# A four-layer conditioned residual stack: another order of the first stage's pieces on GpSimd, VectorE, ScalarE and SyncE, and a pair of layer 0 taken ahead of T2's product

## The chip, the cores and the metric

One core of a Trainium2 chip runs the kernel. The metric is the device time of one execution in microseconds. Its matmuls run on TensorE (PE in the profile, PEld for its weight loads); VectorE is DVE, ScalarE is ACT, GpSimd is POOL, SyncE, which only issues transfers here, is SP.

## What is computed

32 samples of 64 positions and 512 features pass four layers, each with a residual. Layer 0 multiplies by a weight picked by the sample's index, layer 1 is a gated MLP (hidden width 2048) with a low-rank adapter per sample on each of its three matrices, layer 2 a linear map with an adapter, layer 3 again a weight picked per sample:

```python
x = x + einsum('bct,bcd->bdt', x, w0[idx_a]) + bias0[idx_a][:, :, None]
gate = x @ Wg + (x @ Ag[idx_a]) @ Bg[idx_a]
up = x @ Wu + (x @ Au[idx_a]) @ Bu[idx_a]
h = silu(gate) * up
x = x + h @ Wd + (h @ Ad[idx_a]) @ Bd[idx_a]
x = x + x @ W2.T + s[idx_b] * ((x @ A2[idx_b].T) @ B2[idx_b].T)
x = x + einsum('bct,bcd->bdt', x, w3[idx_c])
```

## The kernel before

Every float32 operand of layer 1 is split into a high part (a copy to the matmul's type, by ScalarE: functions ending in `_high`) and a low part (the operand less its high part, by VectorE: functions ending in `_low`). A product is then three matmuls for each 128 rows that are summed over. The gate and up products are done by a two-by-two block scheme with seven products and sums of blocks (Winograd's form of Strassen's): of the activations, blocks B11, B21, B22 and sums T1 to T4, in the slots of the tile XC; of the weights, A11, A12, A22 and S1 to S4, in WC. `XO` (L203) is the order in which XC's slots are filled, and `filled(h, slot)` the semaphore count for it. T3 and T2, T1, T4 are made by `t3_sum`, `t2_sum`, `t1_sum`, `t4_sum` on VectorE, which share two tiles.

The samples are 16 pairs (HP = 8 is half of them) in two halves; the first half's layer 1 starts while layer 0 is still computed for the second. `layer0(p)` on TensorE needs the pair's weight, which GpSimd places by two copies (`place_w0`, L539), its x, which SyncE loads (`load_xin`), and a free bank (`x1_there`: the copy of an earlier pair, `xr_copy` on ScalarE or `xr_sum` on VectorE, has run).

The adapters' input side in the first half: GpSimd selects the samples' columns (`select_a`, L587, four pieces q of four copies each, the matrices' table in RW), `a_high` and `a_low` split them, `adapters_in(0, 0)` takes q = 0 and 1, `adapters_in(0, 1)` q = 2 and 3 (after `a_sum`). `select(h, m)` on TensorE moves the result with small matrices, which GpSimd writes (`move_matrices`, one memset and four casts, semaphore `s_moves`), and `u_own` on VectorE and ScalarE masks it. The output side: the B matrices are loaded (`load_b`), split (`b_high`, `b_low`), stored in a table in DRAM (`store_b`), from which GpSimd gathers the samples' rows into the three places of BL (`gather_b`, three indirect transfers for each half). `lora` on TensorE multiplies them.

Every engine runs its instructions in the order in which its program lists them, and waits on semaphores. For the first stage these orders are written out by hand: SyncE's list of loads, GpSimd's from `pool.wait_ge(s_idx[0], 16)`, ScalarE's from `raw_high(G, 0, ...)`, VectorE's from `g_combine(0)`, TensorE's `first_gate_products` (L1829). The first products are p1 (A11 B11), p6 (S2 T2) and p5 (S1 T1) in three banks, then `c11_product`, `c21_product` and `c12_product`. In `c21_product` the lora waits for the gathered place and the product A22*T4 for `sum_u3`, which has read the same bank. After the gate's seven products come the up's seven, whose weights are combined by `p_combine(0)` on VectorE once `load_u(0)` has landed.

## Time and profile before

| | us |
|---|---|
| median of 3 runs (708.95 to 711.74) | 711.12 |
| profiled execution | 710.6 |
| its span, first to last instruction | 708.8 |
| TensorE busy | 691.5 |
| VectorE busy | 550.3 |
| GpSimd busy | 337.2 |
| ScalarE busy | 268.6 |

The span is what the profile sees; the execution's time is 1.8 us longer. TensorE is busy in 98% of the span, so that its idle pieces, 17.3 us in all, and its clock are what other engines can change. Times of single instructions are in microseconds from the span's start.

### The profile page before, as it was taken

What the parts mean: (1) busy time and instruction counts of PE and PEld (TensorE: products, weight loads), DVE (VectorE), ACT (ScalarE), POOL (GpSimd) and SP (SyncE); (2) the same over time, 40 slices, a digit from 0 to 9 for tenths busy, and PEclk for the clock granted to TensorE, in tenths of its full rate; (3) what the DMA queues carried; (4) which work ended last, traced back from release to release, by engine and by line L of the source; (5) the groups of instructions that cost most, each with busy time, mean ns of one, the idle gap of its engine ahead of it and who ended that gap; (6) DMA issues with size and microseconds to landing.
All of it is one profiled execution on the core that took longest, in us unless ns stands there. A gap on an engine that the chain in (4) does not pass through costs nothing.

```text
span 708.8 us, 10944 instructions
## 1 busy us (share of the span) xinstructions
PE 691.5 (98%) x3667; PEld 592.6 (84%) x3667; DVE 550.3 (78%) x966; ACT 268.6 (38%) x493; POOL 337.2 (48%) x614
## 2 busy tenths in 40 slices
PE   9889999999999999999999999999999999999997
PEld 7768788888888888888778888888888888799997
DVE  8777877888887878699897969696969695975553
ACT  4653513242424242334542323232323231346554
POOL 4875834444344444438356463636343433335541
PEclk9999999999999999999999999999999999999999
DMA  8779724242424232505762332322432225123332
GB/s 215 189 174 212 230 82 134 90 138 85 136 88 148 83 127 82 105 16 164 252 149 85 99 99 90 106 82 80 137 104 81 68 78 184 30 88 114 120 120 97
DMA packets 91895, 84.39 MB, mean 119 GB/s; under 512 B 44736, under 2 KB 73664, under 8 KB 91840
## 3 DMA queue, kind: packets, MB, share of 16 engines
q1 hardware_dynamic: 80128, 52.73, 25.4%
q0 software_dynamic: 11392, 30.95, 14.9%
q8 instruction: 29, 0.48, 0.3%
q14 instruction: 26, 0.21, 0.1%
q10 hardware_dynamic: 320, 0.02, 0.0%
HBM read 70.57 MB, written 13.11 MB: 118 GB/s over the span
## 4 chain that ended last, share of the span: by engine, by line
PE 82%; DVE 7%; POOL 3%; issue 3%; DMA 2%; SPq 1%; ACT 1%; POOLq 0%; DVEq 0%; ACTq 0%
PE bank L1801 40%; PE bank L1932 22%; PE bank L1809 6%; PE bank L1942 4%; PE bank L2068 3%; PE bank L2074 3%; DMA RW<-in_L_cond_Au_dram 2%; PE bank L2047 2%; PE bank L2107 2%; POOL tmp L600 1%; POOL BL L578 1%; DVE XA L1398 1%; DVE hs L1387 1%; DMA BL<-bgtab,poffs 1%; DVE hid L1381 1%
## 5 line engine op out<-in xcount | busy, mean ns | idle before, releaser
L1801 PE MATMUL bank<-XC,WC 128*128 128x512 f32 x1344 | 332.8, 394 | 4.7 <-DVE tmp L1355 2.3
L1801 PEld LDWEIGHTS bank<-XC,WC 128*128 128x128 f32 x1344 | 244.5, 189 | 51.4 <-DVE tmp L1355 3.1
L1932 PE MATMUL bank<-hs,wds 128*128 128x512 f32 x768 | 186.0, 391 | 1.0 <-DVE XA L1398 0.5
L1932 PEld LDWEIGHTS bank<-hs,wds 128*128 128x128 f32 x768 | 141.8, 188 | 29.5 <-DVE wds L1340 0.8
L578 POOL DMA_INDIRECT BL<-bgtab,poffs x96 | 99.3, 1034 | 129.5 <-PE bank L1809 91.3
L578 POOL DMA_INDIRECT BL<-butab,poffs x96 | 98.3, 1024 | 76.4 <-PE bank L1809 55.7
L877 ACT ACTIVATE hs<-hid 128x512 fp32r<-128x512 f32 x64 | 40.1, 629 | 174.7 <-DVE hid L1381 110.3
L1398 DVE TENSOR_TENSOR XA<-bank,XA 128x512 f32<-128x512 f32 x128 | 86.9, 686 | 18.5 <-PE bank L1932 16.8
L871 ACT ACTIVATE hid<-hid 128x512 f32<-128x512 f32 x48 | 30.2, 633 | 149.5 <-DVE hid L1364 79.6
L623 POOL COPY adsel<-ad_raw 128x32 f32 x256 | 46.7, 232 | 59.8 <-DVE ads L1345 59.4
L1809 PEld LDWEIGHTS bank<-UT,BL 128*128 128x128 f32 x384 | 61.5, 190 | 10.5 <-issue 2.4
L1809 PE MATMUL bank<-UT,BL 128*128 128x256 f32 x384 | 66.7, 283 | 2.2 <-DMA BL<-bgtab,poffs 2.2
L1387 DVE TENSOR_TENSOR hs<-hid,hs 128x512 fp32r<-128x512 f32 x64 | 43.8, 690 | 6.7 <-ACT hs L877 5.3
L1942 PEld LDWEIGHTS bank<-hs,ads 128*128 128x128 f32 x256 | 39.1, 189 | 5.2 <-DVE ads L1345 0.3
L1942 PE MATMUL bank<-hs,ads 128*128 128x256 f32 x256 | 40.8, 282 | 0.0
L1313 DVE TENSOR_TENSOR WC<-SC,WC 128x1024 fp32r<-128x1024 f32 x32 | 39.1, 1221 | 0.0
L1381 DVE TENSOR_TENSOR hid<-tmp,hid 128x512 f32<-128x512 f32 x48 | 33.2, 692 | 5.1 <-DVE tmp L1364 0.5
L784 ACT ACTIVATE WC<-SC 128x1024 fp32r<-128x1024 f32 x32 | 33.6, 1051 | 5.6 <-DVE SC L1300 5.6
L1351 DVE TENSOR_TENSOR tmp<-bank,tmp 128x512 f32<-128x512 f32 x32 | 22.0, 687 | 14.6 <-PE bank L1801 14.6
L861 ACT ACTIVATE tmp<-bank 128x512 f32<-128x512 f32 x32 | 19.1, 598 | 31.7 <-PE bank L1801 29.2
L1355 DVE TENSOR_TENSOR tmp<-bank,tmp 128x512 f32<-128x512 f32 x32 | 22.0, 687 | 10.3 <-PE bank L1801 10.3
L1372 DVE TENSOR_TENSOR hid<-bank,tmp 128x512 f32<-128x512 f32 x16 | 11.1, 691 | 22.2 <-PE bank L1809 22.2
(217 smaller groups left out, 867.1 us busy)
## 6 DMA issues: line engine op xcount, KB each, us to landing
RW<-in_L_cond_Wg_dram SPq DMA_DIRECT2D x16, 512.0 KB, 3.5
RW<-in_L_cond_Wu_dram SPq DMA_DIRECT2D x16, 512.0 KB, 3.4
RD<-in_L_cond_Wd_dram SPq DMA_DIRECT2D x16, 512.0 KB, 3.5
out_dram<-XB SPq DMA_DIRECT2D x15, 256.0 KB, 2.1
XB<-in_x_dram SPq DMA_DIRECT2D x8, 256.0 KB, 5.9
x1park<-XB SPq DMA_DIRECT2D x8, 256.0 KB, 6.1
x2park<-XA SPq DMA_DIRECT2D x8, 256.0 KB, 3.1
XA<-x1park SPq DMA_DIRECT2D x4, 512.0 KB, 6.4
```

The source lines that it names most:

```text
L578: nc.gpsimd.indirect_dma_start(BL[:, place, x, :].bitcast(f32), None, btab[b % 2][i], bass.IndirectOffsetOnAxis(poffs[:, at:at + 1].bitcas ...
L623: last = nc.gpsimd.tensor_copy(adsel[:, :, n // DS, n % DS * RANK:(n % DS + 1) * RANK], ad_raw[:, 2 * i:2 * i + 2, bass.ds(col, RANK)])
L784: nc.scalar.activation(WC[:, t, S1:S4 + 1, 0, :, :], SC[:, :, :].rearrange("p s (k f) -> p s k f", k=2), ACT.Copy).then_inc(s_wh[t], 1)
L877: nc.scalar.activation(hs[:, f, 0, t * 512:(t + 1) * 512], hid[:, 2 * f + t, :], ACT.Copy).then_inc(s_hh, 1)
L1313: nc.vector.tensor_tensor(WC[:, t, S1:S4 + 1, 1, :, :], SC[:, :, :].rearrange("p s (k f) -> p s k f", k=2), WC[:, t, S1:S4 + 1, 0, :, :].b ...
L1381: nc.vector.tensor_tensor(hid[:, block_, :], tmp[:, {3: 3, 2: 2, 1: 1}[block_], :], hid[:, block_, :], ALU.mult).then_inc(s_hid, 1)
L1387: nc.vector.tensor_tensor(hs[:, f, 1, at], hid[:, 2 * f + t, :], hs[:, f, 0, at].bitcast(f32), ALU.subtract).then_inc(s_hl, 1)
L1398: nc.vector.tensor_tensor(sums, psD[j % 2][:, :], sums, ALU.add).then_inc(s_evict, 1)
L1801: last = nc.tensor.matmul(psum[:, :], WC[:, t, left, a, k, :], XC[:, right, b, k, :], start=(first and k == 0 and n == 0), stop=(k == 1 an ...
L1809: last = nc.tensor.matmul(psum[:, x * P:x * P + QT], BL[:, b_place(b, tok), x, f * P:(f + 1) * P], UT[:, j, tok, x, :], start=(first and n ...
L1932: last = nc.tensor.matmul(psD[j % 2][:, :], by_feature(wds[:, f, a, :])[:, j % KT, :], hs[:, f, b, j // KT * 512:(j // KT + 1) * 512], sta ...
L1942: last = nc.tensor.matmul(psR[q // 2][:, q % 2 * QT:(q % 2 + 1) * QT], ads[:, f, q, :, :].rearrange("p a m -> p (a m)"), hs[:, f, b, q * Q ...
```

## The change

Five orders are changed. GpSimd writes the moving matrices before anything that needs the indices, places pairs 12 and 13 ahead of the adapters' selection, and selects all four pieces together, ahead of pairs 14 and 15. SyncE stores the first B table ahead of the loads of pairs 14 and 15 and of what follows them. ScalarE takes the sums of the gate's weights earlier and B21 ahead of T2, T3 right behind it. VectorE does the same with the low parts. TensorE takes `layer0(HP + 2)` ahead of p6 instead of behind it.

```diff
-        XO = [[B11, T2, B21, T3, T1, B22, T4], [B11, B21, T3, T2, B22, T1, T4]]
+        XO = [[B11, B21, T2, T3, T1, B22, T4], [B11, B21, T3, T2, B22, T1, T4]]
...
                 load_b(0)
                 for p in range(HP + 2, PAIRS - 2):
                     load_xin(p)
+                store_b(0)
                 for p in range(PAIRS - 2, PAIRS):
                     load_xin(p)
                 load_b(1)
                 load_g(1)
-                store_b(0)
                 load_idx(2, idx_c)
                 load_u(0)
...
                     if p == 0:
+                        pool.wait_ge(s_moves, 1)
                         pool.wait_ge(s_w0i, 1)
                         pool.wait_ge(s_zero, 2)
                     if p == HP:
                         pool.wait_ge(s_zero, 4)
-                    if p == HP + 4:
-                        pool.wait_ge(s_araw, 2)
...
                     if q == 0:
                         pool.wait_ge(s_al, 32 * (h + 1))
-                        pool.wait_ge(s_w0c, PAIRS if h else HP + 4)
-                    if q == 2 and h == 0:
-                        pool.wait_ge(s_w0c, PAIRS - 2)
+                        pool.wait_ge(s_w0c, PAIRS if h else PAIRS - 2)
...
+                pool.wait_ge(s_ident, 1)
+                move_matrices(0)
                 pool.wait_ge(s_idx[0], 16)
...
-                select_a(0, 0, cols)
-                select_a(0, 1, cols)
                 late += adapters(24, 8)
                 for p in range(HP + 4, PAIRS):
                     if p == PAIRS - 2:
-                        select_a(0, 2, cols)
-                        select_a(0, 3, cols)
+                        for q in range(HQ):
+                            select_a(0, q, cols)
                     place_w0(p, late[2 * (p - HP):2 * (p - HP) + 2])
                 pool.wait_ge(s_w0c, PAIRS)
-                move_matrices(0)
                 gather_b(0, 0)
...
                 xc_high(0, B11)
-                for p in range(SUMMED + 1, HP):
+                xr_copy(SUMMED + 1)
+                sums_high(G, 0)
+                for p in range(SUMMED + 2, HP):
                     xr_copy(p)
-                sums_high(G, 0)
+                xc_high(0, B21)
+                xr_copy(HP)
                 xc_high(0, T2)
-                xr_copy(HP)
+                xc_high(0, T3)
                 xr_copy(HP + 1)
-                xc_high(0, B21)
                 a_high(0, 0)
                 a_high(0, 1)
-                xc_high(0, T3)
                 xr_copy(HP + 2)
+                b_high(0)
                 xr_copy(HP + 3)
-                b_high(0)
                 xc_high(0, T1)
...
                 xc_low(0, B11)
+                sums_low(G, 0)
                 t3_sum(0)
                 t2_sum(0)
-                sums_low(G, 0)
+                xc_low(0, B21)
                 xc_low(0, T2)
-                xc_low(0, B21)
+                xc_low(0, T3)
                 a_low(0, 0)
                 a_low(0, 1)
-                xc_low(0, T3)
                 t1_sum(0)
...
                     layer0(HP)
                     layer0(HP + 1)
+                    layer0(HP + 2)
                     pe.wait_ge(s_wl[G], 1)
                     pe.wait_ge(s_xcl, filled(0, T2))
                     p6_product(0, G)
-                    layer0(HP + 2)
                     layer0(HP + 3)
```

## Rows read from the trace of the kernel before

**Rows 1.** The page's part 4: the chain that ended last, by engine.

```profile
PE 82%; DVE 7%; POOL 3%; issue 3%; DMA 2%; SPq 1%; ACT 1%; POOLq 0%; DVEq 0%; ACTq 0%
```

**Rows 2.** TensorE's longest wait from 0 to 90 us: total, times, longest.

```profile
PE bank L1809 <- DMA BL<-bgtab,poffs: 2.2, 1, 2.2
```

**Rows 3.** Timeline of TensorE: start, duration, instructions, idle before and what ended it.

```profile
23.84 1.62 PE L1801 MATMUL bank<-XC,WC 128*128 128x512 f32 x6 [1.42 <-DVE XC L1252]
...
28.23 1.69 PE L1769 MATMUL bank<-XC,UT 128*128 128x256 f32 x12
...
34.56 1.64 PE L1801 MATMUL bank<-XC,WC 128*128 128x512 f32 x6 [0.37 <-DVE XC L1252]
37.02 3.13 PE L1769 MATMUL bank<-XC,UT 128*128 128x256 f32 x24 [0.83 <-DVE UT L1329]
...
51.57 0.66 PE L1809 MATMUL bank<-UT,BL 128*128 128x256 f32 x3 [2.17 <-DMA BL<-bgtab,poffs]
52.03 2.76 PE L1801 MATMUL bank<-XC,WC 128*128 128x512 f32 x6
...
57.02 5.63 PE L1801 MATMUL bank<-XC,WC 128*128 128x512 f32 x24
```

**Rows 4.** Two stretches: length, busy us of the engines, granted clock, DMA share, GB/s.

```profile
18.00:23.80 5.80, 4.42 (x27) 3.59 (x26) 4.91 (x4) 4.07 (x6) 3.47 (x7) 1.00 0.88 215
51.60:56.00 4.40, 4.40 (x16) 3.69 (x17) 3.04 (x5) 0.63 (x1) 0.30 (x1) 0.61 1.02 125
```

**Rows 5.** Timeline of VectorE and ScalarE: t3_sum, T2's low part, a_high, a_low.

```profile
18.75 1.23 DVE L1261 TENSOR_TENSOR hid<-XA 128x1024 f32<-128x1024 f32 x1 [2.20 <-ACT XA L756]
...
22.39 1.30 DVE L1252 TENSOR_TENSOR XC<-hid,XC 128x1024 fp32r<-128x1024 f32 x1
...
26.51 0.63 ACT L809 ACTIVATE BL<-tmp 128x512 fp32r<-128x512 f32 x1 [1.75 <-POOL tmp L600]
...
27.18 0.69 DVE L1329 TENSOR_TENSOR WC<-tmp,BL 128x512 fp32r<-128x512 f32 x1 [0.85 <-ACT BL L809]
```

**Rows 6.** GpSimd's timeline, then its selection copies (ns, min/median/max), one copy alone.

```profile
5.76 1.10 POOL L551 COPY hid<-adsel 64x64 f32 x4 [3.15 <-ACT w3bd L939]
...
15.86 2.75 POOL L551 COPY w0second<-adsel 64x64 f32 x8 [0.72 <-issue]
20.84 5.64 POOL L600 COPY tmp<-RW 128x128 f32 x8 [2.23 <-DMA RW<-in_L_cond_Au_dram]
...
36.84 2.05 POOL L611 CAST WC<-ident 128x128 fp32r<-128x128 f32 x4
39.06 1.15 POOL L578 DMA_INDIRECT BL<-bgtab,poffs  x1 [0.18 <-issue]
...
L600 POOL COPY tmp<-RW x16: 287/418/1283, 20.8 to 32.3; 128x128 f32 x16
...
22.57 1.28 POOL L600 COPY tmp<-RW 128x128 f32 x1
```

**Rows 7.** Timeline of VectorE: sum_u3 of the gate.

```profile
50.04 0.68 DVE L1355 TENSOR_TENSOR tmp<-bank,tmp 128x512 f32<-128x512 f32 x1
```

**Rows 8.** p_combine's start; the store's issue; issues with us to landing; DMA rates, 0:90.

```profile
43.16 0.42 DVE L1295 TENSOR_TENSOR SC<-RW 128x256 f32<-128x256 f32 x1
...
31.54 0.38 SPq L427 DMA_DIRECT2D bgtab<-hs  x1
...
RW<-in_L_cond_Wu_dram SPq DMA_DIRECT2D x1, 512.0 KB, 6.6
...
butab<-hs SPq DMA_DIRECT2D x1, 256.0 KB, 4.9
...
BL<-bgtab,poffs POOLq DMA_INDIRECT x1, 5.2
...
GB/s 3 136 303 350 393 347 120 57 128 273 246 7 117 220 311 182 181 56 115 84 300 266 252 150 93 137 147 200 246 275 358 356 317 309 136 113 295 221 214 97
DMA packets 40584, 18.25 MB, mean 203 GB/s; under 512 B 27520, under 2 KB 37248, under 8 KB 40576
```

## The prediction

> **What bounds the kernel now.** I read four things in this order. The shares of the chain that ended last say which engine sets the time: TensorE has 82% of it [rows 1]. So only two things can move the time here, TensorE's idle time and its clock, and the diff touches only the first 50 us. The list of TensorE's waits there, and its instructions in order of time, give the idle pieces with what ended them [rows 2, 3]: 1.42 us until the low part of T2 (product p6 at 23.84), 0.37 until T1's (p5 at 34.56), 0.83 until the last adapter piece (adapters_in(0,1) at 37.02), 2.17 until the gathered BL rows (51.57). Then the table by stretches, for the granted clock: 1.00 around the 1.42 us wait, 0.61 in the stretch behind the 2.17 us wait, that is part of it at 1.2 instead of 2.4 GHz [rows 4]. The six matmuls of the A22*T4 product took 2.76 us there; its neighbours' 24 took 5.63 [rows 3]. Last, the instructions of VectorE, ScalarE and GpSimd one by one, for what feeds these four waits [rows 5 to 7], and the transfers [rows 8]. Later waits of the kernel follow from TensorE's own progress; I let them move along unchanged.
>
> **T2 and p6.** Before, p6 waited for t3_sum, t2_sum, xc_high(T2), xc_low(T2), ending 23.69 [rows 5]. The first sum waits for the copy of layer 0's eighth pair and starts at 18.75 before and after: nothing moves that. sums_low(G) moves into VectorE's 2.20 us gap ahead of it, since its ScalarE half now runs after xr_copy(5), done near 16.6. xc_low(B21) takes its place ahead of T2's, and xr_copy(HP) stands ahead of xc_high(T2), but TensorE has finished its pair before t2_sum ends. So T2's low part still ends near 23.8. What fills the wait is layer0(HP + 2), about 1.5 us of matmuls; p6 starts near 24.1, followed by layer0(HP + 3) alone, and TensorE is at adapters_in(0,0) at 27.0 instead of 28.23. That would be worth 1.2 us if the adapters' pieces were there.
>
> **GpSimd, where that gain goes.** move_matrices(0) (one memset 0.31 and four casts, 2.05 for these [rows 6]) goes into the 3.15 us in which GpSimd waited ahead of its first placement at 5.76 [rows 6]; it has the matrices done by about 5, with the index load beside it, so the placements of pairs 0 to 7 stay. I cost this at nothing; without that cover it is up to 2.4 us on layer 0's first pairs.
> The placements of pairs 12 and 13 now stand ahead of the adapters' selection. A GpSimd copy takes 0.29 us at the least, but 1.28 when VectorE is in a subtraction of 1024 columns: the copies ran one for each such instruction, each ending just behind it (the one at 22.57 under VectorE's at 22.39) [rows 5, 6]. Twelve copies now stand from 15.86. The first is held as before (16.65), the second by sums_low to 17.9, three run free to 18.8, the next five are held by t3_sum, t2_sum, xc_low of B21, T2 and T3 (20.1, 21.4, 22.5, 23.9, 25.1), two run free to 25.7. The selection begins at 25.85; before it began at 20.84, when its data landed [rows 6]. Each piece is four copies, about 1.0 us, now with VectorE idle: 26.85 and 27.8. Then a_high 0.63 and a_low 0.69 [rows 5] in turn: 27.5, 28.2, 28.5, 29.2. adapters_in(0,0) starts at 29.25, TensorE having idled 2.2 us; before it started at 28.23.
> From there TensorE has 5.9 us (adapters_in and two pairs) to p5, 35.15 against 34.56. T1's low part is ready: the selections of q = 2, 3 end near 31.95 (the copies again one for each of a_low, t1_sum, b_low), then a_sum 0.7 and xc_low(T1) 1.2 give 33.8. xc_low(B22) and two a_low end 36.2, p5 ends 36.6. So adapters_in(0,1) starts at 36.6 instead of 37.02: **0.4 us gained**, the idle 1.42 + 0.37 + 0.83 exchanged for one of 2.2. Bounds: 1.0 us worse, if also the free copies are held; if no placement is held, adapters_in(0,0) starts at 27.0 and VectorE's chain of low parts allows 2.5 us in all.
>
> **BL, the larger part.** Without move_matrices and with the selection in one piece, GpSimd ends placing at about 35.7. The rows of the table need store_b(0): it is issued when b_low(0) ends, 31.05, and its second half took 4.9 us with a 512 KB load ahead of it [rows 8], which is now behind: 36.0. The gathers start there instead of at 39.06 [rows 6]. The one that TensorE waited for was issued 7.2 us after the first one and took 5.2 us [rows 8]: 48.4. TensorE asks at 49.4 - 0.4 = 49.0. So this wait goes. Next late is VectorE's sum_u3, which starts at 50.04 behind u_own(0,5) and takes 0.68 [rows 7]; it starts from TensorE's own last selection and releases the A22*T4 product at 50.78 - 0.4. From there at full clock product, rows, product, rows are 3.5 us: the up products start at 54.3 - 0.4 against 57.02 [rows 3]. sum_c22, which frees the bank for them, moves along and is just in time. **2.7 us gained**, of it 1.2 the wait and 1.5 the clock, since one idle microsecond is left.
>
> **The store ahead of the loads.** In SP's queue store_b(0) is moved past two loads of x (512 KB), and with them load_b(1) (256 KB), load_g(1) (512 KB), the indices and load_u(0) wait for b_low(0). The x of pair 14 lands near 36, needed at 39.5. load_u(0) is needed at 42.7 (p_combine(0), before at 43.16 [rows 8]); behind it on VectorE is u_own(0,0), for which select(0,2) waits. Before, the store was issued at 31.54, the load at about 33, and it landed 6.6 later, 8.1 after the store's issue. With 1.3 MB more in between: 31.05 + 8.1 + 3.5 = 42.7 at the 350 to 390 GB/s of the best slices, 45.5 at the mean 203 [rows 8]. The backlog is dense, so I take the first, and 0.3 us of cost; range 0 to 2.8.
> The Trainium skill (DMA: Bandwidth & Descriptors, Queues, rings and completion order) says that each DMA engine consumes the descriptors of one queue in ring order, which speaks against this edit: every load issued behind the store lands behind it. If order didn't matter, load_u(0) would be in time at any rate. The landings of the trace, in order of issue, agree.
>
> **Sum.** 0.4 + 2.7 - 0.3 = 2.8. The profiled execution took 710.6 (span 708.8), which gives 707.8; the median 711.12 lies 0.5 above it: 708.3. I use the median.
>
> **Rivals.** (1) The new 2.2 us idle at 27 to 29 halves TensorE's clock. For: the 2.17 us one did, and cost about 1.6 us (from 51.57 to 57.02 it is 5.45 us for work of 3.9 at full clock); against: 1.42 us did not, and mine may be shorter. It would take back 1.6: 709.9. Chance 0.3, forecast 0.46. (2) GpSimd is held less than I say, the selection ends early, and TensorE never waits at 27. For: several copies took only 0.3 beside VectorE work; against: the copies at 1.28 [rows 6], one for each of VectorE's long instructions. Up to 2.1 more: 706.2. Chance 0.12. (3) **Slower**: load_u(0) late holds p_combine(0), u_own(0,0) and select(0,2). For: the first gathers now move beside it, and the mean rate gives 45.5. Each microsecond past 42.7 costs one; a stop as long as before's 2.17 us costs the clock's 1.6 too. It decides from a landing at about 44.9 (2.2 + 1.6 against 3.1): then 0.7 slower than before; at 46, 1.8 slower, 712.9. Against: the dense backlog. Chance 0.07 for this, 0.05 for a milder delay (709.5). (4) That the order changes nothing at all (the gathers still late, 711) is in the tails.
>
> **Chances.** 0.5% is 3.6 us, about what a measurement can tell from no change. The forecast lies 0.8 us inside; a third of its chance and most of (2) give faster 0.28; slower by that much needs (3) at its worst: 0.06; within: 0.66. The range runs from (2) to the clock case with a microsecond of delay: 706.2 to 711.2.
>
> **What would show it.** The wait of p6 gone, a wait of 2.2 us at adapters_in(0,0) at 29.2, ended by a_low; the selection starting near 25.8; adapters_in(0,1) near 36.6; the first gather near 36; no wait for BL, one of about 1 us for sum_u3, no stretch at 1.2 GHz there; up products near 54.2. Wrong would be: a DMA wait at p_combine(0), a stretch at half clock after 29, or adapters_in(0,0) ahead of 28.2.

## The result, and the profile after

The changed kernel took 713.42 us (median of 20 runs, 711.6 to 715.75); the kernel before took 710.8 beside it (20 runs, 708.95 to 712.58). The ratio is 1.0034, 95% interval 1.0025 to 1.0044: 2.4 us slower (2.6 by the two medians). The forecast was 708.3 with a range up to 711.2, so the time lies outside it, on the other side of the kernel before. The profiled execution took 714.06 us, its span 712.2, granted clock 0.992. In what follows a ratio leaves out runs that were disturbed as a whole, but a median holds them (two of a_moves_back's 12 took 3894 us, the other ten have a median of 711.26; one of the kernel before's 1381 us in batch 3 and one 1140 us in batch 5).

TensorE's timeline after (start, duration, operation, count, idle before it and what ended it; lines of the file moved up by two or three):

```profile
25.19 1.61 PE L1799 MATMUL bank<-XC,WC 128*128 128x512 f32 x6
...
30.01 1.70 PE L1767 MATMUL bank<-XC,UT 128*128 128x256 f32 x12 [1.89 <-DVE WC L1327]
...
35.92 1.64 PE L1799 MATMUL bank<-XC,WC 128*128 128x512 f32 x6
37.39 3.04 PE L1767 MATMUL bank<-XC,UT 128*128 128x256 f32 x24
...
43.19 1.11 PE L1775 MATMUL bank<-WC 128*128 128x256 f32 x7
44.14 1.55 PE L1799 MATMUL bank<-XC,WC 128*128 128x512 f32 x6
45.81 0.59 PE L1775 MATMUL bank<-WC 128*128 128x256 f32 x3
47.01 0.59 PE L1775 MATMUL bank<-WC 128*128 128x256 f32 x3 [0.61 <-issue]
47.43 0.52 PE L1807 MATMUL bank<-UT,BL 128*128 128x256 f32 x3
50.87 1.19 PE L1775 MATMUL bank<-WC 128*128 128x256 f32 x4 [2.92 <-DVE UT L1408]
51.86 2.76 PE L1799 MATMUL bank<-XC,WC 128*128 128x512 f32 x6
...
56.64 1.66 PE L1799 MATMUL bank<-XC,WC 128*128 128x512 f32 x6 [0.74 <-DVE tmp L1353]
...
60.24 2.00 PE L1799 MATMUL bank<-XC,WC 128*128 128x512 f32 x8
```

Against the kernel before [rows 3], the waits of the first part went as forecast: p6 at 25.19 and p5 at 35.92 have no wait, one wait of 1.89 us stands ahead of adapters_in(0,0), the 0.83 us at adapters_in(0,1) is gone, and so is the wait of 2.17 us for the BL rows at the LoRA products (L1807). What was not forecast stands between: from 45.81 on the matrix selections (L1775) stutter and then stop for 2.92 us, released by VectorE's u_own (L1408). The up products start at 60.24 instead of 57.02, 3.2 us late, and the rest of the kernel keeps that lag: from the start of the up products to the end of the span it is 652.0 us here and 651.8 before.

Why was u_own late? VectorE's timeline of the same execution:

```profile
43.44 0.42 DVE L1293 TENSOR_TENSOR SC<-RW 128x256 f32<-128x256 f32 x1
...
44.97 0.69 DVE L1408 TENSOR_TENSOR UT<-bank,own 128x512 fp32r<-128x512 f32 x1
50.03 1.29 DVE L1408 TENSOR_TENSOR UT<-bank,own 128x512 fp32r<-128x512 f32 x2 [4.37 <-remote]
```

The third selection's matmuls stand at 45.81 for 0.59 us, so they end at 46.40; the u_own that needs only them starts at 50.03, after VectorE had idled 4.37 us. What lies between is the signal from TensorE: its record stands at 50.01, 3.6 us after the matmuls' end. The next selection (end 47.59) and the first rows' product (47.95) are recorded at 50.06 and 50.11, almost together with it. p_combine, at 43.44, is not late (43.16 before [rows 8]), so load_u(0) is not the cause.

The stretches of the clock (length, then busy us and instructions of TensorE, its weight loads, VectorE, ScalarE, GpSimd; then granted clock, DMA share, GB/s):

```profile
7.98:11.39 3.41, 3.41 (x17) 3.41 (x17) 2.91 (x15) 1.53 (x3) 1.42 (x6) 0.50 1.02 352
...
48.94:55.76 6.82, 4.89 (x16) 4.19 (x16) 1.75 (x3) 2.09 (x6) 0.00 (x0) 0.50 1.01 147
```

Two stretches ran at 1.2 GHz (granted clock 0.50): one over layer 0's first pairs, behind a wait of 0.97 us for bias_r at 6.96, and one over the stall and what follows it; before, only the one behind the BL wait did [rows 4]. GpSimd's timeline after, the placements' copies (L550), the selection's (L597), the gathers (L577):

```profile
2.80 1.05 POOL L608 CAST WC<-ident 128x128 fp32r<-128x128 f32 x4
6.07 1.07 POOL L550 COPY hid<-adsel 64x64 f32 x4 [2.21 <-ACT w3bd L936]
...
16.15 10.17 POOL L550 COPY w0second<-adsel 64x64 f32 x12 [1.54 <-issue]
26.55 6.20 POOL L597 COPY tmp<-RW 128x128 f32 x16 [0.23 <-POOL w0second L550]
32.93 3.63 POOL L550 COPY w0second<-adsel 64x64 f32 x4 [0.18 <-POOL tmp L597]
36.86 1.28 POOL L577 DMA_INDIRECT BL<-bgtab,poffs  x1 [0.29 <-POOL w0second L550]
```

### The profile page after: what moved, and what is told of

The parts are those of the page before. It is cut to its first block, busy times and chain, and to the rows that moved or that the text cites. A ratio compares the mean times of both kernels' runs of the same rounds, so it can differ in the third digit from the quotient of the medians.

```text
span 712.2 us, 10944 instructions
## 1 busy us (share of the span) xinstructions
PE 692.7 (97%) x3667; PEld 593.9 (83%) x3667; DVE 549.6 (77%) x966; ACT 268.6 (38%) x493; POOL 337.5 (47%) x614
## 3 DMA queue, kind: packets, MB, share of 16 engines
q0 software_dynamic: 11392, 30.95, 14.8%
## 4 chain that ended last, share of the span: by engine, by line
PE 84%; DVE 8%; issue 3%; POOL 1%; POOLq 1%; ACT 1%; another core or an unknown queue 1%; DMA 0%; SPq 0%; DVEq 0%; ACTq 0%
PE bank L1799 41%; PE bank L1930 22%; PE bank L1807 6%; PE bank L1940 4%; PE bank L2066 3%; PE bank L2072 3%; PE bank L2045 2%; PE bank L2105 1%; PE bank L1767 1%; POOLq L582 1%; DVE XA L1396 1%; POOL w0second L550 1%; DVE hid L1379 1%; DVE XC L1250 1%; DVE hs L1385 1%
## 5 line engine op out<-in xcount | busy, mean ns | idle before, releaser
L577 POOL DMA_INDIRECT BL<-bgtab,poffs x96 | 98.9, 1030 | 130.0 <-PE bank L1807 91.3
L577 POOL DMA_INDIRECT BL<-butab,poffs x96 | 98.8, 1030 | 81.4 <-PE bank L1807 61.0
L1807 PEld LDWEIGHTS bank<-UT,BL 128*128 128x128 f32 x384 | 61.4, 190 | 8.0
L1807 PE MATMUL bank<-UT,BL 128*128 128x256 f32 x384 | 66.5, 282 | 0.0
L1311 DVE TENSOR_TENSOR WC<-SC,WC 128x1024 fp32r<-128x1024 f32 x32 | 38.9, 1217 | 0.0
L2066 PE MATMUL bank<-XC 128*128 128x288 f32 x192 | 28.1, 295 | 0.0
```

The lines of the kernel that those rows point to most:

```text
L577: nc.gpsimd.indirect_dma_start(BL[:, place, x, :].bitcast(f32), None, btab[b % 2][i], bass.IndirectOffsetOnAxis(poffs[:, at:at + 1].bitcas ...
L1311: nc.vector.tensor_tensor(WC[:, t, S1:S4 + 1, 1, :, :], SC[:, :, :].rearrange("p s (k f) -> p s k f", k=2), WC[:, t, S1:S4 + 1, 0, :, :].b ...
L1807: last = nc.tensor.matmul(psum[:, x * P:x * P + QT], BL[:, b_place(b, tok), x, f * P:(f + 1) * P], UT[:, j, tok, x, :], start=(first and n ...
L2066: last = nc.tensor.matmul(banks[:, first, to:to + QT + 2 * RANK], x2t[d % 2][:, a, k, at], W2A[:, b, k, 2 * RANK - w:4 * RANK - w + QT], s ...
```

## The experiments

Five batches of two to four kernels each; the kernels of one batch (the expectations say "call") ran on one chip, beside the kernel before. "Up products" is their start in the profiled execution (57.02 before). "Signals" says whether the records of TensorE's signals stand late in that execution, and whether TensorE's selections stalled with them.

A ratio is not the quotient of the medians beside it: a_again_2 has 0.9977, while its medians give 0.9988. Microseconds worked out from a ratio are good to about 1 us.

| batch | kernel | median us | ratio to before (95%) | up products | signals |
|---|---|---|---|---|---|
| 1 (before 710.91) | a_again | 712.95 | 1.0034 (1.0018 to 1.0051) | 59.00 | late |
| 1 | a_store_back | 712.5 | 1.0026 (1.0012 to 1.0040) | 57.09 | late, one wait of 1.22 |
| 1 | a_moves_back | 711.92 | 1.0014 (0.9987 to 1.0042) | 56.75 | late, no stall |
| 1 | a_ads_late | 712.94 | 1.0023 (1.0004 to 1.0042) | 59.27 | late |
| 2 (before 709.54) | a_gather_held | 710.1 | 1.0009 (0.9997 to 1.0022) | 55.75 | in time |
| 2 | a_pool_sp_back | 709.35 | 0.9997 (0.9984 to 1.0010) | 55.99 | in time |
| 2 | a_sel_moves_back | 709.88 | 1.0005 (0.9995 to 1.0015) | 54.58 | in time |
| 2 | b_moves_early | 709.37 | 0.9998 (0.9988 to 1.0007) | 56.94 | in time |
| 3 (before 710.04) | a_again_2 | 709.16 | 0.9977 (0.9966 to 0.9988) | 55.23 | in time |
| 3 | b_gathers_early | 708.31 | 0.9976 (0.9963 to 0.9989) | 54.02 | in time |
| 3 | a_third_held | 709.24 | 0.9987 (0.9975 to 0.9998) | 54.67 | in time |
| 3 | a_sel_back | 707.42 | 0.9955 (0.9942 to 0.9969) | 53.50 | in time |
| 4 (before 710.02) | a_again_3 | 708.04 | 0.9977 (0.9966 to 0.9989) | 56.80 | in time |
| 4 | b_gathers_early_2 | 708.24 | 0.9974 (0.9963 to 0.9985) | 54.90 | in time |
| 4 | a_third_held_2 | 708.33 | 0.9979 (0.9969 to 0.9990) | 54.95 | in time |
| 4 | a_sel_back_2 | 707.21 | 0.9972 (0.9960 to 0.9984) | 53.68 | in time |
| 5 (before 710.81) | a_again_4 | 712.86 | 1.0027 (1.0013 to 1.0042) | 54.64 | late, no stall |
| 5 | a_sel_back_3 | 712.9 | 1.0026 (1.0013 to 1.0040) | 59.67 | late |

The last column is worked out from the trace: for each of the 585 TensorE instructions of an execution that signal another engine, the time from the matmul's end to the recorded signal. In thirteen profiles (the twelve marked "in time" and the one of the kernel before) none comes over 0.5 us and under 4 us late between 10 and 700 us; in seven (those marked "late" and the first profile of the changed kernel) 33 to 42 do. The one profile of the kernel before is of an execution of 710.6 us that is not among the 20 of the first comparison, and the later batches have none of it; whether its signals come late beside a changed kernel whose signals do isn't known.

Where a signal's own record is missing, the count takes the next one, so 33 to 42 is an upper count. What is real is told by the engine that waits. In after, a_again, a_ads_late and a_sel_back_3 VectorE starts the third selection's u_own 3.6, 1.5, 2.9 and 2.4 us after that selection's end, each time within 0.03 us of a recorded signal. In a_store_back, a_moves_back and a_again_4 it starts 0.04 us after that end, though no record stands there: the signal came and only its record is missing.

One more reading of all twenty profiles: from the start of the up products to the end of the span it is 651.65 to 651.80 us where signals are in time and 651.77 to 652.09 where they are late. So the spans, which go from 705.3 to 712.2 us, differ by what happens ahead of the up products, and late signals behind them cost under 0.5 us.

### Batch 1: which part of the change makes the stall

a_again is the changed kernel once more.

> The changed kernel once more, nothing edited. In its first trace TensorE ends select(0,2), select(0,3) and the first rows' product by 48.0 us, but their signals reach VectorE and the others together at 50.0, and 3.5 us are lost at 47 to 51. If this belongs to the change (theory 1), this trace shows signals of TensorE that come over 1 us late between 43 and 51 again, and the ratio to the kernel before is 1.003 to 1.004. If it was an accident of that one execution (theory 2), the first up product starts near 56 instead of 60.2, though the ratio may still be 1.003 from the clock: two or more stretches at 1.2 GHz.

Both halves came: 1.0034, and the signals late (pair 15's matmuls end at 44.07, its signal is at 45.81), with a stall in two pieces, 0.90 and 1.33 us. Here the wait ahead of adapters_in(0,0) was 2.45 us and the clock did fall behind it, as rival 1 says; in the first profile, behind 1.89 us, it didn't.

a_store_back puts the store of the gate table back behind the loads:

```diff
-                store_b(0)
                 for p in range(PAIRS - 2, PAIRS):
                     load_xin(p)
                 load_b(1)
                 load_g(1)
+                store_b(0)
```

> The changed kernel with the store of the first B table back behind load_g(1), everything else as changed. If the early store, with the loads and gathers pushed into each other behind it, is what costs (theory S), the time falls by 2 us or more below the changed kernel's, to 711 or less, ratio 1.000 or below. If not, the first gathers start later by up to 1 us, still ahead of need, and the time stays within 0.7 us of the changed kernel's.

No stall at its first four selections, up products at 57.09, but 1.0026 in its timed runs: one profile doesn't speak for the runs here. The first gather was issued at 36.69 and took 2.07 us, the second stood at 39.06; then TensorE waited 1.22 us for BL. One signal did come late: the sixth selection ends at 49.13, its signal is at 50.79, and VectorE had idled for it:

```profile
50.82 0.69 DVE L1408 TENSOR_TENSOR UT<-bank,own 128x512 fp32r<-128x512 f32 x1 [3.67 <-remote]
...
52.16 2.93 PE L1799 MATMUL bank<-XC,WC 128*128 128x512 f32 x6 [1.22 <-DVE tmp L1353]
```

sum_u3 stands behind that u_own, and the A22*T4 product waits 1.22 us for it.

a_moves_back puts the zero matrices back ahead of the first gather:

```diff
                     if p == 0:
-                        pool.wait_ge(s_moves, 1)
...
-                pool.wait_ge(s_ident, 1)
-                move_matrices(0)
                 pool.wait_ge(s_idx[0], 16)
...
                 pool.wait_ge(s_w0c, PAIRS)
+                move_matrices(0)
                 gather_b(0, 0)
```

> The changed kernel with move_matrices(0) back behind the last placement. If the matrices in GpSimd's first gap cost something at the start (they held VectorE's small instructions by 0.3 us and with them the bias, theory M), the first product p1 starts 0.3 us earlier and the time falls by 0.3 us or more; otherwise the first gather starts 2.4 us later, near 39.2, and BL's wait of up to 2 us returns: 1 to 2 us slower than the changed kernel.

First gather at 38.87, BL wait 1.95, no stall. Its interval, 0.9987 to 1.0042, holds both the kernel before and a_again: it decides nothing.

a_ads_late tests whether SyncE's issue of the second Ad transfer, which took 4.3 us just where the signals are late (45.68 to 49.98), is what delays them:

```diff
                 for n in range(ADAPTERS):
+                    if n == 1:
+                        sp.wait_ge(s_prod, 6)
                     sp.dma_start(ad_raw[:, :, n * RANK:(n + 1) * RANK],
```

> The changed kernel; SyncE waits for the sixth product signal (near 50 us) before the second of the eight transfers of Ad, whose issue took 4.3 us from 45.7 to 50.0 in the changed trace, exactly until TensorE's late signals arrived. If this issue delays them (theory L), the signals come within 0.1 us of the matmuls' ends, select(0,4) follows by 47.5 instead of 50.9, and the time falls by 2.5 us or more, ratio 1.000 or below. If the cause is elsewhere, the time stays within 0.7 us, or rises when the later Ad transfers come late.

The stall stayed (0.62 and 2.18 us, up products at 59.27), with no such issue beside it. That theory falls; the same issue takes 4.0 us in the kernel before (from 45.42) and 4.9 us in a_again_2, where signals are in time.

### Batch 2: hold the gathers, and single parts

```diff
                 pool.wait_ge(s_w0c, PAIRS)
+                pool.wait_ge(s_prod, 3)
                 gather_b(0, 0)
```

> The changed kernel with one wait more: GpSimd holds its first gather until TensorE's third product of gate 0 (T1's) is through, so about 38.4 us where it was 36.3 to 36.9; the zero matrices stay first and SyncE's store stays early. Theory G (the gathers' transfers, started before 37 us beside the loads that the early store pushed back, make TensorE's signals between 43 and 50 us come late): the late signals go, the matrix selections run as one block without a stall near 46 to 50, up products start near 57.0 instead of 59 to 60.2, and the median falls by 1.5 to 2.5 us to 710.5 to 711.5. Theory P (the late signals come from what the early matrices do at the start, a TensorE that runs about half a microsecond behind the other engines throughout): the signals are late all the same, up products near 59 or later, median near 713. Either way the clock stretch behind the idle at 29 us remains.

The signals were in time and the ratio 1.0009. At the time I read this as theory G confirmed. It isn't: in the other three kernels of this batch no signal was late either, so this batch can't tell what the held gathers did to them. What it does show is the price of late gathers (the first at 39.29) where no signal is late, a BL wait of 1.34 us:

```profile
51.84 0.59 PE L1808 MATMUL bank<-UT,BL 128*128 128x256 f32 x3 [1.34 <-DMA BL<-bgtab,poffs]
```

a_pool_sp_back keeps only the orders of ScalarE, VectorE and TensorE (it undoes the hunks of GpSimd and SyncE).

> Of the change only the orders of ScalarE, VectorE and TensorE: T2 behind B21, the T2 product behind a third pair of layer 0; GpSimd's and SyncE's orders are those of before. My forecast's first term alone: T2's wait of 1.42 us goes, adapters_in(0,0) at 27.0 to 28.5, no idle over 1.5 us before it and so no half-rate stretch there; the wait for BL (2.2 us) and the half-rate stretch behind it near 52 stay as before. Theory O (the order costs nothing by itself): 710.4 to 711.2, ratio 0.999 to 1.001 to before. Rival: the order by itself is the loss, since sums_low and T3's halves ahead of a_low put back what VectorE gives a_low: adapters_in(0,0) at 29 or later, 712 to 713.

Two rows of TensorE's timeline:

```profile
28.05 1.70 PE L1771 MATMUL bank<-XC,UT 128*128 128x256 f32 x12 [1.23 <-DVE WC L1331]
...
36.04 3.14 PE L1771 MATMUL bank<-XC,UT 128*128 128x256 f32 x24 [0.44 <-DVE UT L1331]
```

adapters_in(0,1) starts 0.98 us earlier than before (37.02 [rows 3]), but the ratio is 0.9997: in the timed runs the order alone can't be told from nothing.

a_sel_moves_back undoes all of GpSimd's hunks and keeps the early store.

> The changed kernel with GpSimd's order of before in full (adapter selection behind the twelfth pair's placement, zero matrices at the end), the early store and the orders of ScalarE, VectorE and TensorE kept. The run that had only the matrices back kept a wait of 2.45 us before adapters_in(0,0) and one of 1.95 for BL. If the late selection is what makes that first wait (its copies hold VectorE while it has a_low to write), it is under 1 us here and adapters_in(0,0) starts by 28.5; first gather about 38.9, BL wait 1.5 to 2.2, up products near 56.5, median 710 to 711: the same as before or up to 0.8 us below. If the wait comes from VectorE's own order, it stays near 2 us and the median is 711.5 to 712.

adapters_in(0,0) starts at 28.40 behind 1.23 us, the BL wait is 1.92, the ratio 1.0005. Against a_moves_back's 2.45 us, with the late selection, the wait is half as long: the late selection is its source, as forecast. Behind the 1.92 us its profile has no stretch at half clock.

b_moves_early is the kernel before with the zero matrices first.

> The kernel before with one thing changed: the zero matrices and their copies ahead of the first placement. Forecast's second term alone: first gather near 37, 2 us earlier, the BL wait of 2.17 us under 0.8, up products near 56. Theory G, in the form that needs the early store as well, expects no late signals here and a gain of 1 to 2 us: 709 to 710. If early gathers alone delay TensorE's signals, a stall of 1 to 3 us stands in the selections near 46 to 50 and the median is 711 to 713. If the early copies cost VectorE its small operations (bias_r late at 7 us, half-rate stretch in layer 0's first pairs, as the changed kernel's trace had), that costs up to 1.3 us at 7 to 12 us.

```profile
39.12 1.15 POOL L579 DMA_INDIRECT BL<-bgtab,poffs  x1 [2.64 <-issue]
```

GpSimd was ready 2.64 us early and waited for the stored table: the gathers did not move (39.06 before [rows 6]). The matrices are worth nothing without the store, and with a_store_back the converse holds. Only together do they bring the gathers forward to 36.4 (b_gathers_early below).

### Batch 3: the same kernel, now faster

b_gathers_early is the kernel before with the zero matrices first and the early store, and nothing else of the change. a_third_held holds the third block of gathers, up's:

```diff
+                    if unit == 0:
+                        pool.wait_ge(s_sel, 3)
                     gather_b(b + 1, 0)
```

a_sel_back is the changed kernel with the adapters' selection where it was (the waits that go with its place are left out here):

```diff
...
+                select_a(0, 0, cols)
+                select_a(0, 1, cols)
                 late += adapters(24, 8)
                 for p in range(HP + 4, PAIRS):
                     if p == PAIRS - 2:
-                        for q in range(HQ):
-                            select_a(0, q, cols)
+                        select_a(0, 2, cols)
+                        select_a(0, 3, cols)
```

> The changed kernel, nothing altered, timed beside the three kernels of this call, because the kernel before read 1.2 us lower beside the last four than beside the first four. If the kernels of the last call were near 1.000 for what they had put back, this one stays at 1.003 (1.002 to 1.0045) and its trace shows the late signals again, with gathers from 36.3 to 36.9 on; if it reads 1.001 or less, the ratios of different calls can't be set beside one another.

> The kernel before with the zero matrices first and SyncE's store of the gate table ahead of the last inputs: with the matrices alone the first gather stayed at 39.12 after 2.64 us of idle (the table was not stored), so the two edits together are what brings the gathers to 36 to 37. ScalarE's, VectorE's and TensorE's orders and the selection's place are those of before. Theory G (the time of the gathers alone makes TensorE's signals late): a stall of 1 to 3.5 us in the matrix selections between 45 and 51, up products at 58 or later, ratio 1.002 to 1.004. Rival, that it needs the changed kernel's selection or orders too: no stall, the BL wait under 1 us, up products near 55.5, ratio 0.997 to 0.999.

> The changed kernel with the third block of gathers (up's table, the seventh to ninth, which the changed kernel issues from 45.0 to 47.5) held until TensorE has signalled its third matrix selection; the first six stay at 36.3 to 43. If it is the up table's gathers, at 45 to 48, beside the selections that make the signals late, they are in time here: no stall, no BL wait, up products near 55.5, ratio 0.998 to 1.000, and this is the version that keeps what the change was to bring. If it is the first six, the stall of 2 to 3.5 us stays and the ratio is 1.003.

> The changed kernel with the adapter selection where it was, half behind the twelfth pair's placement; zero matrices and store stay early. adapters_in(0,0) at 28.0 to 28.6 behind a wait of 1.2 to 1.4 us, as in the two runs that had this order, instead of 29.4 to 30.0 behind 1.9 to 2.45. Gathers from about 36.0 on. Theory G: the late signals and a stall of 1 to 3.5 us in the selections stay, ratio 1.001 to 1.003, a little under the changed kernel's because the path is 0.8 to 1.2 us earlier up to the stall. Rival, that the stall comes from the late start of adapters_in: none here, ratio 0.997 to 0.999.

The changed kernel, nothing altered, was faster than the kernel before: 0.9977, which is 1.6 us (0.9 by the medians). Its third selection and u_own, VectorE's row:

```profile
46.99 1.29 DVE L1408 TENSOR_TENSOR UT<-bank,own 128x512 fp32r<-128x512 f32 x2 [0.78 <-PE bank L1775]
```

and TensorE's:

```profile
7.59 1.08 PE L2002 MATMUL bank<-bias_r,bias_of 40*128 40x64 f32 x8 [1.03 <-DVE bias_r L1201]
...
30.64 1.70 PE L1767 MATMUL bank<-XC,UT 128*128 128x256 f32 x12 [1.88 <-DVE WC L1327]
...
43.81 1.11 PE L1775 MATMUL bank<-WC 128*128 128x256 f32 x7
...
46.35 0.94 PE L1775 MATMUL bank<-WC 128*128 128x256 f32 x6
47.82 0.71 PE L1775 MATMUL bank<-WC 128*128 128x256 f32 x4 [0.17 <-DVE UT L1408]
...
51.64 1.66 PE L1799 MATMUL bank<-XC,WC 128*128 128x512 f32 x6 [0.71 <-DVE tmp L1353]
...
55.23 5.63 PE L1799 MATMUL bank<-XC,WC 128*128 128x512 f32 x24
```

From the first selection to the block of four it takes 4.0 us here (43.81 to 47.82) and 7.7 in the first profile (43.19 to 50.87): the late signals cost 3.7 us. To the up products it is 11.4 against 17.1 us, so another 2.0 us go with the clock and the waits behind. The two spans differ by 5.2 us (707.0 and 712.2), and 5.0 of these stand at the start of the up products (55.23 and 60.24), though the first profile was 0.6 us ahead at the first selection. This is the path that the forecast describes: no BL wait, 0.71 us for sum_u3, full clock behind it.

b_gathers_early has up products at 54.02, 3.0 us before those of the kernel before, and 0.9976: the part that brings the gathers forward is the whole gain of the changed kernel. a_third_held (0.9987) neither helps nor hurts by an amount that its interval shows. a_sel_back, with six runs, has the lowest ratio of the study:

```profile
28.18 1.69 PE L1773 MATMUL bank<-XC,UT 128*128 128x256 f32 x12 [1.09 <-DVE WC L1333]
...
36.16 3.14 PE L1773 MATMUL bank<-XC,UT 128*128 128x256 f32 x24 [0.45 <-DVE UT L1333]
...
49.92 1.66 PE L1805 MATMUL bank<-XC,WC 128*128 128x512 f32 x6 [0.72 <-DVE tmp L1359]
...
53.50 5.63 PE L1805 MATMUL bank<-XC,WC 128*128 128x512 f32 x24
```

### Batches 4 and 5: chip or moment

> The changed kernel a third time. One of two: trace with late signals (pair 15's signal after 43.5 with its products' end over 1 us before it, up products at 59 or later) and ratio 1.002 to 1.0045; or trace without (up products near 55 to 56) and ratio 0.997 to 0.9985. Nothing in between if the stall is the whole difference.

> The kernel before with matrices first and the store early, again. Theory G (early gathers make the signals late, where the chip or the moment is such that it happens at all): it shows the stall whenever the changed kernel of this call shows it, ratio then 1.001 to 1.003, and 0.997 to 0.998 otherwise. If it goes without the stall while the changed kernel has it, the gathers' time is not enough and the orders matter.

> The third block of gathers held, again. Where the changed kernel of this call stalls: no stall here if up's gathers are the cause (ratio 0.999), the same stall if the first six are (ratio 1.003). Where it doesn't stall: 0.998 to 0.999.

> The changed kernel with the selection back where it was, again: fastest so far, 0.9955. If the stall comes: selections up to 1.2 us earlier than the changed kernel's, ratio 1.000 to 1.002. If it doesn't: 0.995 to 0.997.

Batch 4 repeats batch 3 on another chip, with overlapping intervals: 0.9977, 0.9974, 0.9979, 0.9972. No signal is late. In a_again_3's profile the wait at adapters_in(0,0) was 2.45 us and the clock stayed at half from 28.7 to 35.6. That is rival 1, and it had its price: from adapters_in(0,0) to p5 it took 8.6 us (29.44 to 38.05) against 5.9 in a_again_2 at full clock, 2.7 us more, and this execution, 710.31 us, was the slowest of the kernel's nine, whose median is 708.04.

> The changed kernel a fourth time. If the late signals go with the chip: on the chip of the first two calls ratio 1.002 to 1.0045 and a stall of 2 us or more in the selections between 45 and 51; on another chip either that, or 0.997 to 0.999 with up products at 55 to 57 and no stall. A ratio near 1.003 with no late signals in the trace, or one near 0.998 with them, would say that the stall is not what separates the calls.

> The selection back where it was, a third time: 0.9955 to 0.9972 so far. Where the changed kernel stalls in this call, this one stalls too if early gathers are enough (its first gather is at 35.9 to 36.0, as early as the changed kernel's), ratio 1.000 to 1.002; where it doesn't, 0.995 to 0.998.

Batch 5 ran on the same chip as batch 4, some minutes later, with late signals and 1.0027 and 1.0026. And batches 1 and 2, on one other chip, differ in the same way. So the chip is not what decides. Within batch 5 two of the changed kernel's 12 runs took 708.49 and 709.1 us and ten 711.4 to 714.8; the profiled one is the 708.49, which lacks records like the others, but where VectorE starts in time (up products 54.64). So none of the ten longer executions has a profile. a_sel_back_3's profile, of 713.53 us, has the stall:

```profile
44.78 0.59 PE L1781 MATMUL bank<-WC 128*128 128x256 f32 x3
46.15 0.59 PE L1781 MATMUL bank<-WC 128*128 128x256 f32 x3 [0.78 <-issue]
...
48.65 1.19 PE L1781 MATMUL bank<-WC 128*128 128x256 f32 x4 [1.54 <-issue]
49.64 2.76 PE L1805 MATMUL bank<-XC,WC 128*128 128x512 f32 x6
...
54.42 2.93 PE L1805 MATMUL bank<-XC,WC 128*128 128x512 f32 x6 [0.74 <-DVE tmp L1359]
```

It shows too that the late selection isn't needed for the stall.

Another thing goes with the late signals, in all seven profiles and in none of the thirteen: records of semaphore updates are missing. 6228 to 6316 are recorded over an execution there, against 8564 to 8571 in the others, and of the 2,299 that a_again_4 lacks against a_again_3, 1,471 (525, 519 and 427) belong to the three semaphores of the BL gathers. It can be seen without counting, in the list of DMA issues from 30 to 44 us, whose last column is the median time from issue to landing. a_again, then a_again_3:

```profile
BL<-bgtab,poffs POOLq DMA_INDIRECT x6
```

```profile
BL<-bgtab,poffs POOLq DMA_INDIRECT x6, 3.8
```

In a_again no landing could be told. The packets themselves are the same in number and median duration (11,392 of the gathers' queue in either), so the packets are not slower; what is late or lost are the messages about them, and the engines' signals beside them. TensorE's are not the only ones: in the first profile 78 of VectorE's 855 and 50 of ScalarE's 431 signals have no record within 0.3 us, in a_again_2 none. A missing record need not mean a late signal: ScalarE's masking ends at 46.86 in the first profile and the next record of its semaphore stands 6.39 us later, but TensorE, which waits for it, went on at 47.01.

## Why the prediction was wrong

**T2 and p6.** The exchange of waits was right, its balance not. p6 has no wait, and adapters_in(0,0) was expected at 29.25 behind 2.2 us; the changed kernel's five profiles give 29.44 (twice), 29.84, 30.01 and 30.64, four of them behind 1.88 to 2.45 us (a_again_4 has 1.36 us ahead of a pair at 23.92 in its place). p6 was forecast at 24.1 and stands at 24.05 in the two profiles whose clock was full up to there and that had no wait ahead of it (a_again, a_again_3). adapters_in(0,1) was to start at 36.6, 0.4 earlier than before; it started at 37.2 to 38.2, and at 39.5 in a_again_3 behind the half clock, later than the 37.02 of before. With the selection back (a_sel_back) it started at 36.16. So the T2 order is worth up to 0.9 us by the trace, and the late selection takes that and more.

**GpSimd.** The selection was forecast at 25.85, it started at 26.55, and at 25.97 in a_again_3, where the first pairs were at full clock. Twelve copies took 10.17 us, 0.85 us each against 0.29 us at the least, which agrees with VectorE's long instructions holding them. The cover of the zero matrices held: the first placement stands at 5.83 to 6.69 in the kernels that have them first, and at 5.76 to 6.21 in the four that don't. What I had not reckoned with is a clock stretch at the very start: four profiles, all of kernels with matrices, store and selection as changed, have a wait of 0.86 to 1.14 us for bias_r at 7 us and half clock from 8 or 9 us on; a_moves_back has the wait (1.19) and not the stretch, so its cause isn't settled. In the first profile p1 starts at 19.23 instead of the 18.09 of a_again, 1.1 us later; the selection's 0.7 us and adapters_in's 0.8 us against the forecast go with this stretch.

**BL and the clock.** The mechanism was right: the first gather at 36.3 to 37.5 (forecast 36), no BL wait, 0.51 to 1.02 us for sum_u3 (forecast 1), no half clock there where no signal was late. It was the last placement that released the first gather (0.29 us ahead of it), not the store, for which I had 36.0: in a_again_3 the two tables landed at 33.5 and 34.5. By the profiles the part is worth its 2.7 us: b_gathers_early's up products start 3.0 and 2.1 us ahead of 57.02. By the runs it is less: b_gathers_early measures 0.9976 and 0.9974, which is 1.7 and 1.8 us, with intervals of about 0.9 us to either side. I had put the clock's 1.5 us in full. But the kernel before hasn't its half-rate stretch in every run: three of its runs in batch 3 (709.01, 709.11 and 710.01 us) show a granted clock of 1.000 over the whole execution. The one profile that I had showed the stretch.

**The store.** The 0.3 us is in the noise. p_combine at 43.44 shows that load_u(0) was in time; in a_again_3, whose records are complete, it landed at 41.5 (forecast 42.7). The nine transfers from the store on landed there in the order of their issue, 33.5 to 41.5, as the prediction had it, without consequence. The Trainium skill (DMA: Bandwidth & Descriptors, Queues, rings and completion order) says only that descriptors are consumed in ring order, and that a later one may finish its write first; that what is issued later also lands later is what the traces show here.

**The sum.** 2.8 us were forecast; batches 3 and 4 gave 0.9977 twice, 1.6 us (0.9 and 2.0 by the medians). The BL term with the store (2.7 - 0.3 = 2.4) measured 1.75 as b_gathers_early, 0.65 less; what is left for T2 and the selection is 1.6 - 1.75 = -0.15 where the sum had 0.4, 0.55 less. These two make the missing 1.2, but each is within the intervals; the second holds the clock stretches at 8 us and behind the wait at 29, of which the latter is rival 1. In those two batches the prediction's 708.3 stands beside 709.16 and 708.04. That it is near is in part luck: the kernel before took 710.04 and 710.02 there and not the 711.12 that the forecast starts from.

**What failed outright.** The step "So this wait goes. Next late is VectorE's sum_u3", which "starts from TensorE's own last selection". It takes TensorE's signals for immediate. They were, in the only profile that I had, that of the kernel before (0 of 585 late). In four profiles of the first comparison and of batches 1 and 5 VectorE got them 1.5 to 3.6 us late in the selections, a stretch where TensorE waits for VectorE and VectorE for TensorE piece by piece, so that each late signal is on the path; TensorE stood 2.92 us and the up products started at 60.24, where my sum has 54.2. In those comparisons the changed kernel takes 712.86 to 713.42 us against 709.16 and 708.04 elsewhere, 3.7 to 5.4 us more. The kernel before takes 710.80 to 710.91 against 709.54 to 710.04, 0.8 to 1.4 us more; why is not shown, as there is no profile of those executions. None of my rivals had this, and rival 3, the only one on the slower side, had another mechanism, which no trace shows.

**What stays open.** Four things. (1) What sets one batch apart from another: not the chip, as batches 4 and 5 show. (2) Whether the changed kernel is hit harder because its gathers run from 36.3 instead of 39.06 us, and so complete among the selections' signals: for it speak that most of the missing records are the gathers', that the two kernels with one of the two edits back (gathers from 38.9, or from the second on at 39.06) had no stall at their first four selections, and their ratios of 1.0014 and 1.0026 against 1.0034; but these intervals overlap, the profile of a_again_4 has early gathers and no stall either, and neither the kernel with held gathers nor b_gathers_early ran in a batch with late signals. It is argued, not shown. (3) Whether a late signal is late at TensorE or on its way; the profile has only the time of arrival. (4) Whether the recording of these events itself takes part in delaying or losing them; no run here tests that.

## What to carry to other kernels

A gain that consists of removing a wait is worth what the next handover on the path allows, and a chain of short pieces passed back and forth between two engines was here the part of the kernel that late signals hit. Compare only what ran in one batch beside the same reference, and repeat the changed kernel in each batch: here the same file was 0.23% faster in two batches and 0.27 to 0.34% slower in three comparisons, each interval clear of 1. And take more than one profile of the kernel before, of executions from the comparison itself. If a version is to be kept, the one with the selection left where it was is the likelier of the two: medians of 707.42 and 707.21 us beside the changed kernel's 709.16 and 708.04 where signals are in time (ratios 0.9955 and 0.9972 against 0.9977 twice, with overlapping intervals), and no worse otherwise (1.0026 beside 1.0027).

## What the runs showed of the hardware

- VectorE got TensorE's signals 1.5 to 3.6 us after the matmuls' modelled end in four profiled executions, with about 2,300 of 8,566 records of semaphore updates missing; in thirteen, with 8564 to 8571 records, none was 0.5 to 4 us late in the count above. In three more, records were missing, the third selection's u_own started in time, and that of the sixth 1.7, 0.9 and 0.2 us late (a_store_back, a_moves_back, a_again_4).
- The length of an idle piece alone doesn't say whether the clock falls (half clock is a granted 0.50, 1.2 GHz). At 24 us a wait of 1.42 us was followed by half clock in b_moves_early and not in the kernel before nor in either b_gathers_early; 2.45 us ahead of adapters_in was followed by it in a_again and a_again_3 and not in a_moves_back; 1.92 us at the BL wait was not, in a_sel_moves_back, and 1.98 was, in b_moves_early. From the one profile of before I had read 2.17 as over and 1.42 as under a limit.
- Waits of 0.86 to 1.14 us at 7 us, in TensorE's first microseconds of work, were followed by half clock from 8 to 9 us on in four profiles; 1.19 us there, in a_moves_back, was not.
